# High and low halves for three more batches, and statistics one place sooner, in a fused attention and expert kernel

## The reference, cut to what matters

```python
qh = (q @ Wq).reshape(B, N, NUM_HEADS, HEAD_DIM).transpose(0, 2, 1, 3)
kh = (kv @ Wk).reshape(B, M, NUM_HEADS, HEAD_DIM).transpose(0, 2, 1, 3)
vh = (kv @ Wv).reshape(B, M, NUM_HEADS, HEAD_DIM).transpose(0, 2, 1, 3)
scores = jnp.einsum('bhnd,bhmd->bhnm', qh, kh) * scale
attn = jax.nn.softmax(scores, axis=-1)
out = jnp.einsum('bhnm,bhmd->bhnd', attn, vh)
...
x = x + jnp.tanh(g_xattn[0]) * _L0_xattn_ref(_layernorm(x, axis=-1), ctx_512, ...)
x = x + jnp.tanh(g_ffn[0]) * _L0_ffn_ref(_layernorm(x, axis=-1), ...)
```

## Time and profile before

| | |
|---|---|
| time, median of 3 runs | 650.98 us (650.44 to 651.57) |
| the profiled execution | 650.87 us, of which 649.0 us is the span of its trace |
| PE busy | 639.7 us, 99% of the span |
| DVE, ACT, POOL busy | 531.2, 389.6, 330.4 us |
| chain of work that ended last | PE 96%, DVE 2%, ACT 1%, issue 1% |
| chunk 0 of attention | about 21 to 58 us |
| chunks 1 to 6 | about 58 to 300 us |
| chunk 7 | about 300 to 339 us, the experts after it |

### The profile page before, as it was taken

How to read it: one execution, slowest core, us unless ns; L and a number is a source line. 1 busy time by engine, 2 the same in 40 slices (tenths; PEclk the granted TensorE clock), 3 DMA queues, 4 the chain that set the end, 5 groups by cost and what they waited for, 6 DMA issues and landing times.

```text
span 649.0 us, 14075 instructions
## 1 busy us (share of the span) xinstructions
PE 639.7 (99%) x3765; PEld 484.5 (75%) x3765; DVE 531.2 (82%) x1362; ACT 389.6 (60%) x739; POOL 330.4 (51%) x388
## 2 busy tenths in 40 slices
PE   8999999999999999999999999999999999999998
PEld 6657776677766777667658888787887878788786
DVE  6889989888898888988878969788695967869565
ACT  3565766667666676675565565555655555565554
POOL 4335553435534355343404656566565655657563
PEclk9999999999999999999999999999999999999999
DMA  6243233232332323323326565352646435374550
GB/s 183 66 108 83 66 99 86 60 85 60 96 86 60 85 60 96 86 60 83 85 66 172 128 134 135 84 127 85 163 114 134 141 76 130 87 162 115 134 146 17
DMA packets 58429, 65.60 MB, mean 101 GB/s; under 512 B 26256, under 2 KB 35344, under 8 KB 58384
## 3 DMA queue, kind: packets, MB, share of 16 engines
q1 hardware_dynamic: 58384, 65.07, 39.8%
HBM read 61.64 MB, written 2.88 MB: 99 GB/s over the span
## 4 chain that ended last, share of the span: by engine, by line
PE 96%; DVE 2%; ACT 1%; issue 1%; DVEq 0%
PE bank L1291 17%; PE bank L1292 17%; PE bank L1293 17%; PE bank L1391 11%; PE bank L1415 9%; PE bank L1338 5%; PE bank L1358 3%; PE bank L1367 2%; PE bank L1361 2%; PE bank L1364 2%; PE bank L1378 2%; DVE halves L880 1%; PE bank L1381 1%; PE bank L1379 1%; PE bank L1298 1%; ACT halves L628 1%
## 5 line engine op out<-in xcount | busy, mean ns | idle before, releaser
L602 POOL TENSOR_TENSOR halves<-area,halves 128x512 fp32r<-128x512 f32 x134 | 174.4, 1301 | 138.0 <-ACT halves L759 132.5
L780 ACT ACTIVATE area<-bank 128x512 f32<-128x512 f32 x136 | 81.4, 598 | 111.0 <-PE bank L1293 108.7
L1247 DVE TENSOR_TENSOR bank<-area,bank 128x512 f32<-128x512 f32 x128 | 88.5, 692 | 50.8 <-PE bank L1293 50.5
L697 ACT ACTIVATE area<-bank 128x512 f32<-128x512 f32 x128 | 69.5, 595 | 100.2 <-PE bank L1367 100.2
L1291 PE MATMUL bank<-x2t_hi,w_hi 128*128 128x512 f32 x272 | 110.3, 406 | 0.1
L1292 PE MATMUL bank<-x2t_hi,w_lo 128*128 128x512 f32 x272 | 107.3, 394 | 0.0
L1293 PE MATMUL bank<-x2t_lo,w_hi 128*128 128x512 f32 x272 | 106.3, 391 | 0.0
L759 ACT ACTIVATE halves<-area 128x512 fp32r<-128x512 f32 x136 | 85.1, 626 | 17.3 <-DVE area L1258 16.0
L889 DVE TENSOR_REDUCE row_max<-bank 128x4 f32<-128x512 f32 x128 | 82.1, 685 | 8.3 <-PE bank L1338 7.4
L1258 DVE TENSOR_TENSOR area<-bank,wbc 128x512 f32<-128x512 f32 x128 | 86.2, 679 | 0.3 <-DMA wbc<-rows_dram 0.2
L529 POOL TENSOR_TENSOR ctx_hi<-ctx_raw,ones_col 128x128 fp32r<-128x128 f32 x32 | 13.9, 435 | 137.7 <-DMA ctx_raw<-ctx_t 106.8
(11 more groups left out here) (164 smaller groups left out, 1262.6 us busy)
## 6 DMA issues: line engine op xcount, KB each, us to landing
wbc<-rows_dram SPq DMA_DIRECT2D x126, 256.0 KB, 4.3
inverse_bc<-inverse_dram SPq DMA_DIRECT2D x64, 256.0 KB, 3.8
w_raw<-experts SPq DMA_DIRECT2D x32, 102.0 KB, 2.0
x_sb<-x SPq DMA_DIRECT2D x8, 256.0 KB, 3.3
ctx_raw<-ctx_t SPq DMA_DIRECT2D x32, 64.0 KB, 3.3
ctx_keys<-ctx_nat SPq DMA_DIRECT2D x32, 64.0 KB, 2.0
out<-area SPq DMA_DIRECT2D x7, 256.0 KB, 3.9
max_rows<-max_t SPq DMA_DIRECT2D x64, 4.0 KB
```

The lines of the kernel that those rows point to most:

```text
L602: nc.gpsimd.tensor_tensor(hid_lo[:, u % SLOTS, :], hid[:, u % HIDS, :], raw(hid_hi[:, u % SLOTS, :]), ALU.subtract).then_inc(hidlo_ready, 1)
L697: nc.scalar.activation(probs_t[:, k, :, :], st_ps[q][:].rearrange("p (h n) -> p h n", h=4), ACT.Exp)\
L780: nc.scalar.activation(silu_g[:, u % 2, :], gate_ps[u % 2][:], ACT.Silu).then_inc(silu_ready, 1)
L1247: nc.vector.tensor_tensor(up_ps[u % UPS][:], silu_g[:, u % 2, :], up_ps[u % UPS][:], ALU.mult)\
```

## The change

`in_halves` now decides the form of the weighted sum of half 0. It is true for batches 2 and 3 of chunk 0 (`HALVED_FROM = 2`), for all of chunks 1 to 6 as before, and for batch 29, the second of chunk 7 (`HALVED_LAST`). `halved_before` counts how many halved batches came earlier, for the semaphores. In chunk 7, the high half of the first expert input (`x2t_high(0, 0)`) moves on ACT from batch 29 to batch 30, since it overwrites p_lo, and POOL holds the last weight split until batch 29's sum is done. `STATS_AT` gives the statistics of chunks 2 and later one place sooner, so that the last place has none.

```diff
-STATS_AT = {2: (2,), 3: (3, 4), 4: (5,), 5: (6,), 6: (7,)}
+STATS_AT = {1: (2,), 2: (3,), 3: (4, 5), 4: (6,), 5: (7,)}
 X_AT = {0: (5, 6, 7)}
-HALVED_FROM = CB
+HALVED_FROM = 2
+HALVED_LAST = NB - 3
...
+        def in_halves(t, b, first, last):
+            return t == HALVED_LAST if last else not first or b >= HALVED_FROM
+
+        def halved_before(t, last=False):
+            return t - HALVED_FROM - (1 if last else 0)
...
 # POOL
-                    if not first and not last:
-                        split_keys(b, t, c)
+                    if in_halves(t, b, first, last):
+                        split_keys(b, t, c, last)
+                    if last and b == CB - 1:
+                        pool.wait_ge(u_done, 4 * HALVED_LAST + 2)
...
 # ACT
-                    if not first and not last and b % 2 == 1:
+                    if in_halves(t, b, first, last) and b % 2 == 1:
                         probs_high(t)
-                        if b == 1:
+                        if b == 1 and not last:
                             xt_high(c + 1)
...
-                    if not first and not last and b % 2 == 0:
+                    if in_halves(t, b, first, last) and b % 2 == 0:
                         probs_high(t)
...
-                    if last and b == 1:
+                    if last and b == 2:
+                        act.wait_ge(u_done, 4 * HALVED_LAST + 2)
                         x2t_high(0, 0)
...
 # DVE
                         if h == 0 and not first:
                             batch_stats(t - CB, b)
+                        if h == 0 and b > 0 and in_halves(t, b, first, last):
+                            probs_low(t, last)
...
 # PE, and the same with q = 1
-                    if first or last:
+                    if in_halves(t, b, first, last):
+                        weigh_halves(t, b, 0, last)
+                    else:
                         weigh(t, b, 0, 0, c + 1)
-                    else:
-                        weigh_halves(t, b, 0)
```

More of the change, by code:

```diff
@@ L533, in split_context, with split_keys @@
                     .then_inc(ctx_ready, 1)
-            def split_keys(b, t, c):
+            def split_keys(b, t, c, last=False):
                 pool.wait_ge(keys_in[b], 16 * c + 16)
-                wait(pool, u_done, 4 * (t - 2) + 4)
+                if not isinstance(t, int) or t > HALVED_FROM + 1:
+                    wait(pool, u_done, 4 * (t - 2) + 4)
                 nc.gpsimd.tensor_tensor(keys_hi[:, b % 2, :], ctx_keys[:, b, :], ones_col[:].broadcast_to([P, 3 * CD]),
                                         ALU.mult).then_inc(keyshi_ready, 1)
-                pool.wait_ge(keyshi_ready, t + 1 - HALVED_FROM)
+                pool.wait_ge(keyshi_ready, halved_before(t, last) + 1)
                 nc.gpsimd.tensor_tensor(keys_lo[:, b % 2, :], ctx_keys[:, b, :], raw(keys_hi[:, b % 2, :]), ALU.subtract)\
@@ L702, in probs_high @@
                 act.wait_ge(exp_ready, 4 * t + 2)
-                wait(act, u_done, 4 * t - 2)
+                act.wait_ge(u_done, 4 * t - 2)
                 for q in range(2):
@@ L891, in take_max, with probs_low @@
                     .then_inc(max_ready, 1)
-            def probs_low(t):
+            def probs_low(t, last=False):
                 for q in range(2):
-                    dve.wait_ge(phi_ready, 2 * (t - HALVED_FROM) + q + 1)
+                    dve.wait_ge(phi_ready, 2 * halved_before(t, last) + q + 1)
                     wait(dve, u_done, 4 * (t - 1) + q + 1)
@@ L1368, in scores, with weigh_halves @@
                                      start=False, stop=True).then_inc(st_done, 1)
-            def weigh_halves(t, b, q):
+            def weigh_halves(t, b, q, last):
+                before = halved_before(t, last)
                 if q == 0:
-                    pe.wait_ge(keyslo_ready, t + 1 - HALVED_FROM)
-                pe.wait_ge(phi_ready, 2 * (t - HALVED_FROM) + q + 1)
+                    pe.wait_ge(keyslo_ready, before + 1)
+                pe.wait_ge(phi_ready, 2 * before + q + 1)
                 wait(pe, u_ready, 4 * (t - 1) + q + 3)
@@ L1379, in weigh_halves @@
                 nc.tensor.matmul(ps, keys_lo[:, b % 2, cols], p_hi[q], start=False, stop=False)
-                pe.wait_ge(plo_ready, 2 * (t - HALVED_FROM) + q + 1)
+                pe.wait_ge(plo_ready, 2 * before + q + 1)
                 nc.tensor.matmul(ps, keys_hi[:, b % 2, cols], p_lo[q], start=False, stop=True).then_inc(u_done, 1)
@@ L1490, in attention @@
                     scores(t, b, 2 * c + b // 2, 1, 2 * c + b // 2 + 1, None)
-                    if first or last:
+                    if in_halves(t, b, first, last):
+                        weigh_halves(t, b, 0, last)
+                    else:
                         weigh(t, b, 0, 0, c + 1)
-                    else:
-                        weigh_halves(t, b, 0)
                     if b % 2 == 1 and not last:
                         g_project(b // 2, c + 1, ((max_ready, 4 * (t + 2) + 3), (exp_ready, 4 * t + 3)))
-                    if first or last:
+                    if in_halves(t, b, first, last):
+                        weigh_halves(t, b, 1, last)
+                    else:
                         weigh(t, b, 0, 1, c + 1)
-                    else:
-                        weigh_halves(t, b, 1)
             pe.wait_ge(neg_ready, 2)
```

## The result

The changed kernel takes 654.50 us, median of 7 runs (653.58 to 657.93), beside 650.98 us for the kernel before, median of 7 (650.44 to 651.59). The ratio is 1.0060, with an interval of 1.0045 to 1.0074: slower, by 3.5 us. The forecast was 652.6 with a range up to 653.3. The direction was right, the size was not. The profiled execution took 654.5 us, with a span of 652.5 (649.0 before).

The account below looks back on a forecast made before the run. PE, busy 639.7 of 649.0 us, was taken to bound the kernel. The terms 1.94 - 0.15 - 0.17 + 0 + 0 = +1.62 us gave a median of 652.6 us, range 650.5 to 653.3.

Parts of the forecast that it names:

- Batch 29 ... Term: 0: Chunk 7: PE saves 0.30 us, then loses it waiting 0.68 instead of 0.38 before the transposition at 320.75; net 0.
- the subtractions fall in that wait and are hidden: Chunk 7, batch 29: DVE's subtractions, 1.22 us, fit in its 2.32 us wait for a transfer until 316.50.
- Batch 2, "1.94 us late": Chunk 0: DVE waits for p_hi, delaying its second take_max; PE reaches max_scores of batch 5, half 0, 1.94 us late.
- Batch 3: 1.79 forecast: Chunk 0: PE's max_scores of batch 5, half 1, starts at 53.10 instead of 51.31, 1.79 us late.
- From chunk 0 on: 1.62 forecast: After batch 3's q = 0 part saves 0.17 us, PE stays 1.62 us late, unchanged through chunks 1 to 6.
- The rival that p_hi isn't late: Batch 2: DVE meets p_hi within about 0.2 us, so not slower, 650.2 or 649.9 us at best; chance 0.17.
- The statistics: 0: Chunk 0 on DVE: moving the statistics one place sooner costs nothing by itself.
- The clock rival: Batch 2: PE's new 2.2 us wait drops its clock, adding 2.5 us: sum 4.1, 655.1 us; chance 0.08.
- PE's saving of 0.30 us a batch: Even batches: the halved sum takes PE 1.56 us against 1.86 in f32, saving 0.30 us.

Follow-up runs that it names:

- e3: The kernel before with halves in batch 29 alone, HALVED_FROM and STATS_AT as before: 653.11 us, ratio 1.0031.
- e5: The kernel before plus POOL's key split of batch 29, whose result nobody reads; PE, ACT and DVE keep the f32 form: 652.92 us, ratio 1.0029.
- e4: e3 with POOL's key split of batch 29 waiting only for batch 27's half 0 sum, so it starts earlier: 652.02 us, ratio 1.0009.
- e1: The kernel before with only the new STATS_AT places of the statistics: 651.29 us, ratio 1.0005.
- e8: e4 with the low half of the first expert input moved behind the last weight split on POOL: 651.68 us, ratio 1.0006.
- e14: e8 with POOL's weight split of place b = 2 in the last chunk also waiting until DVE has written xn: 651.63 us, ratio 1.0007.
- e16: e11 with POOL's weight split of place b = 2 in the last chunk also waiting until DVE has written xn: 651.58 us, ratio 1.0006.
- e2: The changed kernel with batch 29 in f32 as before, so chunk 0's part alone: 654.61 us, ratio 1.0045.
- e10: The whole change plus both POOL edits of e8 in the last chunk: 654.15 us, ratio 1.0039.
- e15: The changed kernel with only POOL's weight split of place b = 2 in the last chunk also waiting for xn: 656.15 us, ratio 1.0073.
- e6: e2 without statistics in place 4; those of chunks 6 and 7 stay in places 5 and 6: 652.98 us, ratio 1.0024.
- e11: The changed kernel with batch 2 left in f32 (halves in batches 3 and 29) and both POOL edits of e8: 652.12 us, ratio 1.0007.

## Why the prediction was wrong, and where it was right

**The step that failed: "Batch 29 ... Term: 0".** It measured 2.1 us alone (e3), and 1.66 in chunk 7 of the change's profile. Two things were wrong in it. The change adds a key split to POOL there as well, which also holds back the weight split and the bias behind it, and the prediction costed POOL's splits for chunk 0 only, where a wait of 7.21 us covers them. In chunk 7 POOL's own time is free too, but DVE's iteration runs at the same moment, and it is stretched from 2.55 to 3.63 us. e5 shows this split, with what stands behind it on POOL, costing 1.9 us, and e4, which only moves it, takes the ratio from 1.0031 to 1.0009. And "the subtractions fall in that wait and are hidden" is true of the subtractions (316.70 and 317.29 after, in front of a wait of 1.01), but not of what is delayed ahead of the reciprocal, since that wait is 5.3 to 5.8 us of transfer behind the reciprocal, whenever this comes.

For two engines that slow each other, the rows show a block, not a sharing: DVE's first operation, begun at 305.94 beside a POOL operation that runs from 305.85 to 306.45, lasts 0.54 us and ends at 306.48, and in the kernel before POOL's split, begun at 309.81 under the last of xn's operations, with DVE's product of two tiles right behind it at 309.85, lasts 1.64 us and the product its usual 1.21. The Trainium skill ("SBUF — State Buffer", Terms and SBUF: two separate sides) has this rule: VectorE and GpSimd share a pair of ports as an exclusive lock for a whole instruction, "the loser fully blocks", where VectorE's operation uses both ports or has two inputs in SBUF. The trace agrees. It was the rule that spoke against this change, and the prediction didn't weigh it.

**Batch 2, "1.94 us late": right in kind, 1.83 measured** (47.22 - 45.63 = 1.59, and the start of chunk 0 was 0.24 ahead). The subtractions began at 43.19, not 43.54, since all stood 0.26 earlier; from there to the second `take_max` it is 2.64 us, as worked out. **Batch 3: 1.79 forecast, 1.33 + 0.24 = 1.57 measured** (52.64 - 51.31). **From chunk 0 on: 1.62 forecast, 1.39 measured**, and flat over chunks 1 to 6 as said. The rival that p_hi isn't late is refuted by the wait of 1.66 us.

**The statistics: 0, and 651.29 beside 651.00 measured** (e1): right.

**The clock rival, 0.08, had too small a chance.** Its argument against, that PE's waits of 0.28 and 0.38 us leave the clock alone, says nothing of a wait of 2.1. In the change's own runs it shows once in 7; in kernels with the same wait in 12 of 17. Its price was set at 2.5 us; the levels are 1.6 to 1.9 apart, and PE's order shows 0.9 to 1.4 in chunk 0. It is not in the profile after, so it is no part of the 3.5 us there.

**A term that the prediction didn't have: 0.68 us behind chunk 7.** It put the cost of chunk 0 at what PE is late behind `g_project`, and nothing after that. In all ten kernels with halves in chunk 0, and in none of the other eight but e8, DVE stands more than 1 us for the sums' transfer before the inversion at 346.62 (1.09 to 1.38 us; 0.19 at most in the seven others), and PE's lateness grows by 0.33 to 0.69 us at the product behind it (0 in the seven others). e8's profile, whose clock had fallen some 20 us ahead, has a wait of 1.94 and 0.22 of growth. Why the transfer lands late in those kernels wasn't found.

**The sum by what the runs show:** by PE's order in the change's profile -0.24 at the start, 1.39 in chunk 0, 1.66 in chunk 7 and 0.68 behind it, 3.5 us. By the kernels with one part each: chunk 0 alone 1.9 us where the clock holds (two runs), batch 29 alone 2.1 us; together 4.0. The ranges of the parts are wider than the difference.

**What stays open.** PE's saving of 0.30 us a batch shows in no end time: with nearly all the costs mended (e8, e14, e16) the kernels are level with the kernel before or 0.4 to 0.6 us above it. What makes the sums' transfer behind chunk 7 late isn't known. The spread of some 2 us within one kernel, at full clock, isn't settled either. Not tried was p_hi of batch 2 ahead of ACT's copy at 42.04, the order that would shorten the wait of 1.66 us itself.

## What to carry to other kernels

An engine with idle time isn't free: before giving POOL work in its idle stretch, look at what DVE does in the same microseconds, above all in chains of small operations, and at what those release. A wait for a transfer hides only what stands behind the transfer's start; what comes ahead of the instruction that starts it is paid in full. And a wait of TensorE of 2 us may be paid a second time in its clock, in some executions only, so one profile at 1.00 doesn't clear it.

## What the runs showed of the hardware that was not expected

- Of two operations of DVE and POOL that meet, one has its usual time, and the other's row is longer, not preceded by idle time: POOL's split of 128x204 takes 0.53 us alone and 1.64 beside DVE's product of 64x1024 (1.21); DVE's operation on 128x24 takes 0.16 alone and 0.54 beside POOL's of 0.60, and ends 0.03 us after it. A busy row that has grown is the sign to look for.
- The same wait of TensorE, 2.09 to 2.11 us, left the granted clock at 1.00 in one profile (the change) and took it to 0.50 to 0.56 in the next 2 us in others (e2, e10, e15). In e8's profile a wait of 2.27 us was followed by 0.50 too; waits of 1.70 to 1.86 us were followed by 1.00 (e3, e6, e10, e11).
